# 103 products without a reader in eight pauses of TensorE

## What is computed

```python
def reference(x, src, dst, ...):
    edge_index = jnp.stack([src, dst])
    deg = jnp.maximum(jax.ops.segment_sum(jnp.ones(dst.shape, jnp.float32), dst, num_segments=384), 1.0)
    x = x + _L0_gnn_ref(_layernorm(x, axis=-1), edge_index, ...)         # attention over the edges, 8 heads
    x = x + _L0_ffn_ref(_layernorm(x, axis=-1)[None])[0]                 # the shifter
    x = x + _L1_gnn_ref(_layernorm(x, axis=-1), edge_index, ...)         # three graph convolutions with a graph norm
    x = x + _L1_ffn_ref(_layernorm(x, axis=-1)[None], w_up, w_down)[0]   # two layers of quantised weights
    x = x + _L2_gnn_ref(_layernorm(x, axis=-1), edge_index, W, b)        # one more convolution
    x = x + _L2_ffn_ref(_layernorm(x, axis=-1)[None], ...)[0]            # 6 experts, each token goes to one
    x = x + _L3_gnn_ref(_layernorm(x, axis=-1), src, dst, deg, ...)      # mean over neighbours, layer norm
    x = x + _L3_ffn_ref(_layernorm(x, axis=-1)[None], ...)[0]            # 64 experts, 8 per token
    return x
```

## Time and profile before

| | us |
|---|---|
| median of 3 runs | 889.49 |
| lowest and highest | 886.07, 890.65 |
| the profiled execution | 888.59 |
| its span, first to last instruction | 886.9 |
| TensorE busy with matmuls | 640.7 (72%) |
| VectorE busy | 532.8 (60%) |
| mean granted clock of TensorE | 0.831 |

### The profile page before, as it was taken

How to read it: one execution, slowest core, us unless ns; L and a number is a source line. 1 busy time by engine, 2 the same in 40 slices (tenths; PEclk the granted TensorE clock), 3 DMA queues, 4 the chain that set the end, 5 groups by cost and what they waited for, 6 DMA issues and landing times.

```text
span 886.9 us, 9573 instructions
## 1 busy us (share of the span) xinstructions
PE 640.7 (72%) x2855; PEld 311.0 (35%) x2878; DVE 532.8 (60%) x1472; ACT 277.4 (31%) x1103; POOL 229.4 (26%) x232
## 2 busy tenths in 40 slices
PE   5952424433234850998588998848999999999997
PEld 3420112111112750445335554433344344344332
DVE  3457988679697979444635225664447844445533
ACT  2104755456563330333504011111222222222222
POOL 5154776676772721000000000001011011111100
PEclk9985556665555965999598999969999999999999
DMA  8599486776875707900300000285999999999991
GB/s 337 229 384 320 132 260 214 237 245 190 276 211 202 249 1 257 383 1 8 135 0 1 0 1 0 80 326 203 405 418 412 406 395 408 419 408 417 417 364 38
DMA packets 46502, 208.08 MB, mean 235 GB/s; under 512 B 7953, under 2 KB 12561, under 8 KB 36848
## 3 DMA queue, kind: packets, MB, share of 16 engines
q1 hardware_dynamic: 27152, 145.70, 41.5%
q0 software_dynamic: 19296, 61.75, 20.9%
HBM read 199.67 MB, written 10.31 MB: 237 GB/s over the span
## 4 chain that ended last, share of the span: by engine, by line
PE 48%; DVE 6%; DMA 4%; ACT 1%; issue 1%; DVEq 0%; POOLq 0%; SPq 0%
PE bank L835 11%; PE bank L863 6%; PE bank L855 6%; PE bank L725 4%; PE bank L740 3%; DMA R<-tok_tab,slot_tok 3%; PE bank L646 3%; PE bank L539 2%; PE bank L640 2%; PE bank L824 2%; PE bank L534 1%; PE bank L747 1%; DMA R<-L_w 1%; PE bank L695 1%; PE bank L768 1%
## 5 line engine op out<-in xcount | busy, mean ns | idle before, releaser
L583 PE MATMUL bank<-R 128*128 128x384 bf16 x144 | 50.0, 483 | 141.1 <-DVE R L1258 106.7
L960 ACT ACTIVATE R<-R 128x128 f32<-128x128 f32 x384 | 113.3, 296 | 103.2 <-DVE R L1297 73.6
L835 PE MATMUL bank<-R 128*64 128x512 f32 (+1 forms) x432 | 106.6, 602 | 0.5 <-ACT R L1050 0.5
L492 POOL DMA_INDIRECT R<-tok_tab,slot_tok x33 | 33.2, 1006 | 269.6 <-DVE slot_f L1657 212.2
L539 PE MATMUL bank<-R,late 128*128 128x512 f32 x168 | 79.8, 635 | 0.0
L960 ACT ACTIVATION_READ_ACCUMULATOR R<-R 128x1 f32 x384 | 72.1, 188 | 14.7 <-issue 14.6
L583 PEld LDWEIGHTS bank<-R 128*128 128x128 bf16 x144 | 13.3, 119 | 173.1 <-DVE R L1258 125.5
L863 PE MATMUL bank<-R 128*128 128x512 bf16 x284 | 68.5, 380 | 3.6 <-issue 1.9
L1669 DVE TENSOR_TENSOR R<-R,bank 128x256 f32<-128x256 f32 x34 | 14.3, 420 | 90.9 <-ACT R L1062 90.9
L1293 DVE TENSOR_TENSOR R<-R 128x1032 f32<-128x1032 f32 x48 | 59.0, 1229 | 15.8 <-DMA R<-tab_dst,e_i 12.0
L450 POOL DMA_INDIRECT score<-late,e_i x48 | 57.4, 1196 | 42.4 <-DVE late L1252 25.4
(11 more groups left out here) (371 smaller groups left out, 1163.4 us busy)
## 6 DMA issues: line engine op xcount, KB each, us to landing
R<-L_w SPq DMA_DIRECT2D x54, 1536.0 KB, 10.7
late<-L_w SPq DMA_DIRECT2D x18, 1536.0 KB, 9.6
R<-L_w SPq DMA_DIRECT2D x2, 3072.0 KB, 15.2
score<-R POOLq DMA_DIRECT2D x9, 512.0 KB, 11.8
R<-score SPq DMA_DIRECT2D x3, 1536.0 KB, 10.1
R<-L_Ww SPq DMA_DIRECT2D x2, 2048.0 KB, 12.5
R<-L_W SPq DMA_DIRECT2D x4, 1024.0 KB, 9.0
tab_src<-R SPq DMA_DIRECT2D x3, 516.0 KB, 3.0
```

Source lines behind the costliest of these rows:

```text
L583: last = pe.matmul(pb[s][:, 0:N], oh[:, e % 2, 0, P * s:P * s + P], oh[:, e % 2, 1, :], start=(e == 0), stop=(e == ET - 1))
L835: last = pe.matmul(pb[4 + i % 2][part, :], xeT[i % 2][:, k, part], w13[e % NWB][:, k, :], start=(k == 0), stop=(k == KD - 1), tile_positio ...
L960: act_.activation(own, own, ACT.Copy, accum_out=w_e3[:, t, h:h + 1]).then_inc(S("heads_summed"), 1)
```

## The change

A helper on TensorE's stream issues a given number of bf16 products of 128x128 ones by the identity repeated four times, 512 columns each, into a PSUM bank that nothing reads until a real product with `start=True` has overwritten it. It is called at eight places. The first call stands behind a wait for the shifter's three additions on GpSimd, the others have no wait of their own. No other engine's stream changes.

```diff
--- before.py
+++ after.py
@@ -540,6 +540,10 @@
                                      start=(k == chunks_[0]), stop=(k == chunks_[-1]))
                 return last
 
+            def keep_busy(bank, products):
+                for _ in range(products):
+                    pe.matmul(pb[bank][:, :], onesb[:, :], identb[:, None, :].to_broadcast([P, D // P, P]), start=True, stop=True)
+
             pe.wait_ge(S("consts_ready"), 1)
 
             for t in range(NT):
@@ -625,6 +629,8 @@
                 attend(i, NT - 1)
 
 
+            pe.wait_ge(S("shifter_added"), NT)
+            keep_busy(7, 14)
             for t in range(NT):
                 transposes("3", t).then_inc(S("xT_psum"), 1)
             for l in range(3):
@@ -657,6 +663,7 @@
                         last.then_inc(S("h_out_psum"), 1)
 
 
+            keep_busy(6, 16)
             for t in range(NT):
                 pe.wait_ge(S("bitq_ready"), t + 1)
                 for k in range(KD):
@@ -670,6 +677,7 @@
                 for k in range(KD):
                     last = pe.matmul(pb[3 + t][:, 0:F1], xqT[:, k, P * t:P * t + P], wuq[:, k, :], start=(k == 0), stop=(k == KD - 1))
                 last.then_inc(S("bit_psum"), 1)
+            keep_busy(6, 10)
             for t in range(NT):
                 pe.wait_ge(S("bitq_ready"), NT + t + 1)
                 for c in range(2):
@@ -682,6 +690,7 @@
                 last.then_inc(S("bit_psum"), 1)
 
 
+            keep_busy(6, 11)
             for t in range(NT):
                 transposes("5", t).then_inc(S("xT_psum"), 1)
             pe.wait_ge(S("weights_loaded"), 80)
@@ -696,6 +705,7 @@
                 last.then_inc(S("graph5_psum"), 1)
 
 
+            keep_busy(7, 13)
             pe.wait_ge(S("rows_loaded"), 96)
             pe.wait_ge(S("weights_loaded"), 80)
             for t in range(NT):
@@ -778,10 +788,12 @@
             pe.wait_ge(S("sage_used"), 2)
             transposes("8", 1).then_inc(S("xT_psum"), 1)
             logits(1)
+            keep_busy(5, 8)
             pe.wait_ge(S("sage_used"), NT)
             transposes("8", 2).then_inc(S("xT_psum"), 1)
             logits(2).then_inc(S("router_psum"), 1)
 
+            keep_busy(5, 26)
             pe.wait_ge(S("picked_ready"), 1)
             for t in range(NT):
                 for s in range(t + 1):
@@ -863,6 +875,7 @@
                         last = pe.matmul(pb[t][:, :], spread[i % NSM][:, P * t:P * t + P], y_part[i % 2][c], start=(i == 0 and c == 0), stop=(i == NTILE - 1 and c == 2), skip_group_check=True)
                 last.then_inc(S("combined"), 1)
 
+            keep_busy(5, 5)
             pe.wait_ge(S("slot_onehot"), 2 * NT)
             find_part(1, 0, 1, F3).then_inc(S("slots_psum"), 1)
             pick_first_tokens()
```

## The result

The changed kernel takes 883.24 us (median of 20 runs, 877.57 to 890.57), the kernel before 887.28 us beside it (20 runs, 884.59 to 893.75). The ratio, with its 95% interval, is 0.9946 [0.9923, 0.9969]: 4.8 us, or 0.54%, faster. (The two medians lie 4.0 us apart, within that interval.) The profiled execution took 884.42 us, with a span of 882.7; the one of before took 888.59.

A forecast was written before the change was run, and what follows sets the result against it. From 325 to 604 us the chain alternates between TensorE and short VectorE and ScalarE norm chains, so faster matmuls shorten it. Terms -0.5 - 0.4 - 2.1 - 2.6 + 1.0 = -4.6 us from 889.49 gave 884.8, range 881.9 to 888.4.

The forecast's parts named there:

- Stretch 1: 14 products before norm 3's transposes, from the shifter's end: 0 us, bounds -1.3 and +0.5.
- Stretch 2: 16 products in the 4.41 us pause before the bit-linear layer's transposes: -0.5 us, bounds -0.8 and 0.
- Stretch 3: 10 products in the 2.89 us pause before the hidden rows' transposes: -0.4 us, bounds -0.8 and +0.5.
- Stretch 4: 11 products in the 3.46 us pause before norm 5's transposes: -2.1 us, bounds -2.2 and -0.6.
- Stretch 5: 13 products in the 3.89 us pause before norm 6's transposes: -2.6 us, bounds -2.8 and -1.0.
- Stretches 6 to 8: 8, 26 and 5 products at the router: it speeds up, but whatever is won becomes pause before the gathered rows.
- The longer pause: Wait for gathered rows grows by up to 2.5 us, clock down when work resumes: +1.0 us, bounds 0 and +1.7.
- What would show it: List of expected profile signs, including the gathered-rows wait growing from 3.15 to over 5 us, clock down at its end.
- this luck neither comes nor goes with the change: Quick clock rise after stretch 1 in the profiled kernel before, about half of 1.7 us, taken as unaffected.
- rival A: Clock survives the longer pauses too, in stretch 1 and before the gathered rows: 882.6 us, chance 0.14.
- B: Rival: pauses left after stretches 4 and 5 and one-by-one transposes lose the clock, halving the gain there: 887.2 us, chance 0.27.
- C: Rival: unread products do not count as work for the clock and run at half clock, slower: 892.5 us, chance 0.07.

The follow-up runs named there:

- e4: Changed kernel with 24 products instead of 14 in stretch 1 and 22 more before the first tile's gathered rows; 877.42 us, ratio 0.9896 to the kernel before.
- e2: Changed kernel with products only in stretch 1 and stretches 6 to 8, none in stretches 2 to 5; 886.37 us, ratio 1.0014 to the kernel before.
- e3: Changed kernel with all 103 products cut from 512 columns to one, calls, wait and order kept; 885.62 us in one run.
- e11: The kernel before, unchanged, run and profiled a second time; 869.28 us.
- e1: Changed kernel with products only in stretches 2 to 5; 882.03 us against 885.35 for the kernel before, ratio 0.9943.
- e5: Kernel before, no products, with SyncE's three token stores issued ahead of the four expert-weight loads; 868.21 us against 874.70, ratio 0.9967.
- e6: Changed kernel with SyncE's three token stores issued ahead of the four expert-weight loads; 862.51 us, ratio 0.9875 to the kernel before.
- e12: The changed kernel, unchanged, run and profiled a second time; 872.66 us.
- e7: Changed kernel with half the products at all eight places; 870.13 us in one run, beside 874.70 for the kernel before.
- e8: e6 with 24 products instead of 14 in stretch 1; 863.76 us, ratio 0.9867 to the kernel before.
- e9: e8 without the products of stretches 6 to 8; 863.43 us in one run, beside 873.34 for the kernel before.
- e10: e8 with 36 products instead of 26 at one router place; 871.30 us in one run, beside 873.34 for the kernel before.

## Why the prediction was right

It said 884.8 us (881.9 to 888.4) and the kernel took 883.2, with 4.8 us to the kernel before where 4.6 was forecast. The 884.8 stood on three runs of the kernel before (889.49), which over twenty has 887.28. By its steps, in the two profiles and from the shifter's end:

- **Stretch 1, 0:** as forecast. The clock rose at 349.80, 4.7 us into the products, they ended 2.60 us early, and it fell at 353.20 under the transposes. The aggregation starts 0.22 us later than before. e4 showed the other side: with the pause closed it is worth 1.5 us. (In e2 the same 14 products happened to bring 2.12 us for the transposes, and nothing behind them: 22.62 for the aggregation.)
- **Stretch 2, -0.5, bounds -0.8 and 0:** mis-sized. The hidden rows' transposes come 0.91 us sooner although the aggregation started 0.22 later, which makes -1.1, outside its bound. The step that failed is "VectorE then has three tiles of 0.8 each". In before a tile starts on VectorE every 0.79 to 0.86 us (428.90, 429.69, 430.55), in VectorE's timeline of after every 0.66 us:

```profile
428.84 0.29 DVE L1515 TENSOR_SCALAR R<-R 128x256 f32<-128x256 f32 x1 [1.70 <-ACT R L1020]
...
429.50 0.28 DVE L1515 TENSOR_SCALAR R<-R 128x256 f32<-128x256 f32 x1
```

VectorE begins on the first tile 0.58 us sooner and is 0.33 us faster over the three, and together that is the 0.91. Part of the miss is the profile of before: from the aggregation to these transposes it takes 66.12 us, e2, e3 and e11 65.8 and after 64.99, so that against those three the gain is 0.8.

- **Stretch 3, -0.4:** -0.4 (at norm 5 the gain has grown from 0.91 to 1.32).
- **Stretch 4, -2.1:** -2.0 (from 1.32 to 3.31 at norm 6). The transposes took 1.63 us and the passes 10.51.
- **Stretch 5, -2.6:** -2.35 (from 3.31 to 5.66 at the six experts).
- **Behind that, nothing forecast:** from the six experts to the first gathered tile 0.7 us came back (127.47 in before, 128.16 in after). All traces with the stores in their old place lie between 126.6 and 128.6 there, and I have no cause for these 0.7.
- **Stretches 6 to 8, nothing:** right, by e1 and e2. The reason was right too: the path goes over the token store. The 2.6 us for the 24 passes at full clock was too low; they take 2.94.
- **The longer pause, +1.0:** +1.24 (first to third tile 9.14 in before, 10.38 in after), with the pause at 6.00 us and the clock down, as "What would show it" had it. That the longer pause is the reason is not shown: e1 pays the same with a pause of 2.35 us.

So the terms are right to 0.3 us but for stretch 2, and its miss of 0.6 was made up by the 0.7 and 0.2 us that no term had. That leaves 3.7 us at the third tile, and the 4.7 at the end has the 1.0 of scatter from the expert loop in it. That the sum came so close is in part luck.

**Two statements were wrong.** The first is "this luck neither comes nor goes with the change". In five traces without working products in stretches 2 to 5 (before, e2, e3, e5, e11) the six experts start 131.73 to 133.95 us after the shifter, in four with the products of stretches 2 to 5 (after, e1, e6, e12) 125.87 to 126.10. The products take away not only the half clock but also the chance in when it ends, and the profile of before was one of the lucky ones. The mean of the five is 132.8 and of the four 125.9, so the gain at this point is about 6.9 us and not 5.7. Behind it 1.3 us come back: from the six experts to the end before, e2, e3 and e11 take 410.2 us on the mean (409.9 to 410.7), after, e1 and e12 take 411.5 (411.3 to 411.6). That leaves 5.6, and the times say 4.8 (2.8 to 6.8 us by the interval of the ratio).

The second is the ground given against rival A, "2.60 us lost it", taken as if a pause of that length always did. It did twice in after; in e7 pauses of 2.59 and 3.10 us were survived, and in e12 the one of 2.59 at the router. The Trainium skill ("TensorE: Matmul & The Clock Gate", "Why this matters for your kernels") tolerates short pauses, and these are of the order it means; by that e7 agrees and after disagrees, with its falls at 353.20 and 581.90, and so do e4, e8 and e9, with falls behind pauses of 1.1 us at most. What separates them stays open. It is not the work just before: ahead of the 2.58 us that lost the clock in after stood 26 products at full clock in 5.78 us, and the same 26 stood ahead of the 2.59 us that kept it in e12. (One sentence of the working has its numbers the wrong way round: the window of 0.68 holds 0.64 us at 1.2 GHz and 0.36 at 2.4. The edges drawn from it are right.)

**The rivals.** A did not come: the clock was lost in stretch 1 and at the gathered rows. B did not come in after: 1.80 and 1.08 us of pause held it, as in every trace with the full counts, and so did transposes with pauses of 0.8 to 1.1 us between them. But it was a real rival: in e4, e8 and e9 the clock fell at just these transposes, and with it falls the prediction's "a pause under 1.6 us is safe as far as this trace goes". C, that unread products do not count, is refuted from both sides: by after, where 16 of them run in 3.62 us, and by e3, where the same instructions without their columns bring nothing. On the transposes the weighing in the prediction stands: the twelve of norm 6 took 1.54 us with the clock up and 2.79 with it down. Whether transposes by themselves would hold the clock is another question, which no run here answers.

## What to carry to other kernels

Where an engine's clock depends on its own work, fill its pauses on the critical path with work that ends just before the next real instruction is ready, and size the filling by that remainder: here 14 products did nothing where 24 gave 1.3 to 1.5 us at the next block. Look also at the thin stretches behind it, where short pieces of work alternate with pauses: in three of four traces the clock fell there and took most of that gain back. Before filling, follow the chain one stage on: what is won ahead of a transfer becomes a wait, and the clock can fall in it again; move the transfer first, and the same products pay. Read gains from a fixed event behind the noisy stage, and take two traces of each kernel, since a single one has its luck in it.

## What the runs showed of the hardware

- Products whose result is never read held TensorE's clock like any others: 16 in 3.62 us in stretch 2, with 0.96 us of pause behind them. The same instructions with one column, 14 in 0.53 us, left the pause as it was, and the clock fell in it.
- When half clock ends differs from one execution of the same kernel to another: the 24 f32 passes of norm 5 took 11.35 us in one trace and 11.95 in another, against 10.51 with the clock held.
- Pauses of 2.58 and 2.60 us lost the full clock (after) and pauses of 2.59 (e7, e12) and 3.10 us (e7) kept it. It also fell with no pause above 1.1 us behind 16 products at full clock (e4, e8, e9), where the same pauses kept it in after, e1, e6, e10 and e12; and of 1.52 and 1.50 us one lost it (e9) and one kept it (e8).
- A store of token rows that stands behind four loads of 1.5 MB each in one queue landed 18.9 us after its issue; the change of order that took it off the chain gave 4.8 us in the traces, with no byte saved (by the times 0.9967 [0.9929, 1.0005]).
